# A transformer and mixture-of-experts kernel on one core: biases of q, k and v folded into weights made on chip, one more head on VectorE, shared first products in another order

## The chip, the core and the metric

The kernel runs on one core of a Trainium2 chip. Five engines work side by side and meet at semaphores: PE (TensorE, matrix products), DVE (VectorE), ACT (ScalarE), POOL (GpSimd) and SP (SyncE, which here only issues DMAs). The metric is the device time of one execution in microseconds (us); the time of the kernel before is the median of three executions.

## The reference

Input is 16 x 512 tokens of 256 numbers in float32. What is computed, cut to what matters:

```python
xn = layernorm(layernorm(x)) * ln1_w + ln1_b          # the inner norm has no weights
q, k, v = xn @ wq + bq, xn @ wk + bk, xn @ wv + bv    # 16 heads of 16
fq, fk = elu(q) + 1, elu(k) + 1
kv = einsum('bhnd,bhne->bnde', fk, v)                 # sum over the heads h of one token
attn = einsum('bhnd,bnde->bhne', fq, kv) / (einsum('bhnd,bnd->bhn', fq, fk.sum(1)) + 1e-6)
x2 = layernorm(x) + attn @ wo + bo
x1 = x + x2 + gelu(LN2(x2) @ fc_w + fc_b) @ proj_w + proj_b
h = layernorm(x1)
out = x1 + shared(h) + sum over the top 2 of 8 experts of weight * expert(h)
# shared(h) = (silu(h @ sg_gate.T) * (h @ sg_up.T)) @ sg_down.T; an expert has the same form
```

Attention stays within a token: for each token the 16 heads of q meet the 16 heads of k and v, so it is elementwise work of 16 x 16 x 16 products, done on DVE and POOL and not on PE.

## The kernel before

The 8192 tokens go through in 16 blocks of 512, each of four tiles of 128 tokens. A block passes through a pipeline of stages, one per round of `body(c, j)`: in round c the attention of block c is computed (`core`), block c-1 gets its output product, LN2 and the MLP (`stage_b`), block c-2 is routed to experts and gets the first products of the shared expert (`stage_c`), and block c-3 gets the shared expert's last product and is stored (`stage_d`). Projections of the first three tiles of block c+1 stand in round c already (`more`). Rounds 0 to 18 take about the first 1140 us. Then the tokens, sorted by expert in HBM, go through the experts in 71 tiles of 256 rows. That second phase is not touched.

Every engine has its own list of instructions, written out by hand in the order in which it runs them, and waits at semaphores where it needs another's result. So an engine that waits holds up all that stands behind in its own list.

What the change and the prediction touch, by lines of the kernel before:

- PE, `project_x(c, u, part)` (L1448 on): part "T" transposes a tile u (L1456, identity as weights); part "P" multiplies it with `wqkv_sb` into PSUM, 512 columns for q and k and 256 for v (L1466), and then adds the biases with two bfloat16 products of `bias_rows_bf` and `bias_bf` (L1471), one of 512 and one of 256 columns. "P" waits for `pq_free`, with which DVE gives back the PSUM bank.
- PE, `body`: the output product with `wo_sb` (`to_tokens`, L1494, biases L1497), logits (L1626, 16 products of 8 columns), `down` (L1494 with `sgdn_sb`: the shared expert's last product, which waits for `shared_h`), the MLP's first product (L1548), its second (L1494 with `proj_sb`), and `shared_up` (L1641: six first products n = 0 to 5 of the shared expert, gate and up parts in turn).
- ACT, `take_x` (L669 on): takes a transposed tile from PSUM and applies LN1's weight and bias per column (L676, two instructions for the two halves of 128 columns). `take_qkv` (L687, L690, L700) takes q, k (as exp) and v. `take_shared` (L762) takes the six first products, the gate parts through Silu. Silu and exp need different function tables, so `table` (L772) and `table_exp_ln` (L776) load one.
- DVE, `heads` of a tile by `own_heads(u)`: 16, and for tile `SPLIT` = 2 only 16 - `POOL_HEADS`. Four long instructions per tile make its attention: `products_qk` (L1026), `sums_1` (L1035), `products_2` (L1050), `sums_2` (L1063). `residual_1` (L1144) adds the output product to the residual and waits for `wo_psum`. `weights` (L1211) waits for ACT's `gap_exp`. `features(c + 1, 0)` (L1002, L1007) writes `fqk_pool`, the tile that POOL does alone.
- POOL, `body`: products of that tile (`scores`, L537), sums by halving (L523, L533), `gate_shared` (L583: silu part times up part of the shared expert, whose end is `shared_h`), the second products (L544), the heads of tile SPLIT that are POOL's (`heads`), and eight scatters of rows to HBM (L574).

The lines that say the split and the biases:

```python
POOL_HEADS = 6
def own_heads(u):
    return HEADS - POOL_HEADS if u == SPLIT else HEADS
```

Of the kernel before, what the change touches and what calls it, by code (L numbers as in the profile page):

```python
# [56 lines left out]

POOL_TILE = 3
SPLIT = 2
POOL_HEADS = 6  # L60
RANKS_AT = 5
ORDER = (POOL_TILE, 0, 1, 2)
BIAS_ROWS = (0, 64, 96)
# [4 lines left out]
def build(nc, x, wqkv, b_tok, ln1w, ln1b, ln2w, ln2b, wo, fc_w, fc_b, proj_w, gate_w, sg_up, sg_down,  # L68
          experts, out):
    ctx = ExitStack()  # L70
    with ctx:
        def sb(name, shape, dt=FP32):
            return ctx.enter_context(nc.sbuf_tensor(name, shape, dt))

        def sem(name):
            return ctx.enter_context(nc.semaphore(name))
# [5 lines left out]


        wqkv_sb = sb("wqkv_sb", [P, KC, 3 * D])
        wo_sb = sb("wo_sb", [P, KC, D])
        fc_sb = sb("fc_sb", [P, KC, MLP])
        proj_sb = sb("proj_sb", [P, FCH, D])
# [5 lines left out]
        ln_sb = sb("ln_sb", [P, 4, KC])  # L93
# [5 lines left out]
        ident = sb("ident", [P, P])  # L99
# [98 lines left out]
            (0, HEADS * HH), (HEADS * HH, 2 * D), (HEADS * HH + 2 * D, D), (HEADS * HH + 3 * D, HEADS * HEADS)))  # L198
        first_v2 = first_v2.rearrange("p (h e) -> p h e", h=HEADS)
        first_s2 = first_s2.rearrange("p (h g) -> p h g", h=HEADS)  # L200
        first_v = sg_u[:, 0, 0:D].rearrange("p (e g) -> p e g", e=HD)


# [51 lines left out]
        xnT_ready = sem("xnT_ready")  # L255
        qkv_psum = sem("qkv_psum")
        qkv_taken = sem("qkv_taken")
        feat_ready = sem("feat_ready")
        pq_free = sem("pq_free")
        pool_v_used = sem("pool_v_used")  # L260
# [111 lines left out]
        def announce(eng, ins, s, value):  # L372


            ins.then_inc(s, 1)
            eng.wait_ge(s, value)
# [17 lines left out]
        def stages(c):  # L394

            return (not isinstance(c, int) or c < BLOCKS, not isinstance(c, int) or c < BLOCKS - 1,
                    *(not isinstance(c, int) or s <= c < BLOCKS + s for s in (1, 2, 3)))

        block = ctx.enter_context(nc.Block())

# [266 lines left out]
        def _(act):  # L667
            a = nc.scalar

            def take_x(c, u):  # L670

                n = 4 * c + u
                wait(act, xT_psum, n + 1)
                wait(act, qkv_psum, n - 1)
                for k in range(KC):
                    ins = a.activation(xnT[u % 2][:, k, :], p_xT[:, k * P:(k + 1) * P], ACT.Identity,  # L676
                                       bias=ln_sb[:, 1, k:k + 1], scale=ln_sb[:, 0, k:k + 1])
                ins.then_inc(xnT_ready, 1)

            def take_qkv(c, u):  # L680
# [137 lines left out]
            def token_numbers(c, j):  # L818
# [2 lines left out]
                act.wait_ge(tok_moved, c - 1)  # L821
                a.activation(rows[j % 2][:, :, C_TOK], tok[:], ACT.Copy).then_inc(tok_written, 1)

            def take_sums(i, dst, src):

                act.wait_ge(first_pool, i + 1)
                a.activation(dst.rearrange("p h g -> p (h g)"), src[:, 0:HEADS * HEADS], ACT.Copy).then_inc(s_taken, 1)

            def body(c, j):
# [62 lines left out]
                if stage_b and (more or not core):  # L892
                    for k in range(2):
                        ln3_sums(c, j, k)
                        ln3_finish(c, k)
                if more:
                    take_qkv(c + 1, 1)
                if stage_c:
                    table(ACT.Silu)
                    take_shared(c, range(2))  # L900
                    if stage_b and not core:
                        normed_rows(c, j + 1)
                    if core and not more:
                        ln3_sums(c, j, 0)
                    take_shared(c, range(2, 4))
                    if core and not more:
                        ln3_sums(c, j, 1)
                if more:
# [64 lines left out]
        def _(dve):  # L973
# [110 lines left out]
            def first_block():  # L1084
# [50 lines left out]
                announce(dve, ins, attn_ready, 1)  # L1135
                dve.sem_inc(pq_free, 1)

            def residual_1(c):
# [83 lines left out]
            def body(c, j):  # L1222
# [17 lines left out]
                if core:  # L1240
                    totals(1, den_1[:, 0:HEADS])
                    products_2(c, 1, False)
                if stage_c:
                    choose(c, j)
                if core:
# [73 lines left out]
            done(v.memset(neg_1[:], -1.0))  # L1319
            done(v.memset(eps_1[:], EPS))  # L1320
            done(v.memset(block_1[:], float(BLOCK)))
            done(v.memset(eps_2[:], EPS * EPS))
            announce(dve, v.memset(act_tmp[:], 0.0), tmp_ready, 1)
            dve.wait_ge(pool_const, 4)
# [121 lines left out]
        def _(pe):  # L1446
            t_ = nc.tensor

            def project_x(c, u, part):

                n = 4 * c + u
                if part == "T":
                    wait(pe, xhat_ready, TPB * c + u + 1)
                    wait(pe, xnT_ready, n)
                    for k in range(KC):
                        ins = t_.transpose(p_xT[:, k * P:(k + 1) * P],  # L1456
                                           xin[:, ORDER[u], k * P:(k + 1) * P], ident[:])
                    ins.then_inc(xT_psum, 1)
                else:
                    wait(pe, xnT_ready, n + 1)  # L1460
                    wait(pe, qkv_taken, n)
                    wait(pe, pq_free, n - 1)
                    parts = ((p_qk[u % 2], 0, 512), (p_v, 512, 768))
                    for bnk, lo, hi in parts:
                        for k in range(KC):
                            t_.matmul(bnk[:, 0:hi - lo], xnT[u % 2][:, k, :], wqkv_sb[:, k, lo:hi],  # L1466
                                      start=k == 0, stop=False)
                    if isinstance(n, int) and n == 0:
                        pe.wait_ge(bias_ready, 1)
                    for bnk, lo, hi in parts:  # L1470
                        ins = t_.matmul(bnk[:, 0:hi - lo], bias_rows_bf[:], bias_bf[:, lo:hi],  # L1471
                                        start=False, stop=True)
# [28 lines left out]
            def body(c, j):  # L1501
# [23 lines left out]
                                    lambda t: wait(pe, rows_ready, TPB * (c - 2) + t + 1))  # L1525
                if core:
                    project_x(c, 2, "P")
                if stage_c:
                    logits(c)
                if stage_d:  # L1530
# [24 lines left out]
                if stage_b:  # L1555
                    wait(pe, gelu_ready, FCH * c - 1)
                    wait(pe, out_ready, c - 2)
                    if stage_c and more:
                        wait(pe, ranks_read, c - 1)

                    def next_x(u):
                        project_x(c + 1, u, "T")
                        if u == 1:
                            project_x(c + 1, 0, "P")
                    to_tokens(hid, FCH, proj_sb, (p_b0, p_b1), 4 * D, proj_psum,
                              at_last_chunk=lambda: wait(pe, gelu_ready, FCH * c),
                              between=next_x if more else None, per_bank=True)
                elif more:
                    project_x(c + 1, 0, "T")
                    project_x(c + 1, 1, "T")  # L1570
# [218 lines left out]
```

## Time and profile before

| | |
|---|---|
| time, median of 3 executions | 1746.89 us (1745.64 to 1747.42) |
| profiled execution, its own time | 1744.85 us |
| its span, first to last instruction | 1742.7 us |
| PE busy | 1680.7 us (96%) |
| DVE, POOL busy | 1166.9 us each (67%) |
| ACT busy | 904.1 us (52%) |
| granted PE clock, mean | 0.985 of full |

DVE and POOL are busy in the rounds of the first phase and nearly idle in the experts' phase, so their share of the whole span says little: a round is to be read by itself. Rows of the timeline give start, duration, engine, line and operation, tiles written and read, the number merged, and in brackets how long the engine had been idle before and what ended that.

### The profile page before, as it was taken

The numbers are of one execution on the slowest core, as the hardware profiler recorded it, in microseconds if no ns is written. First come the engines' busy times: TensorE is split into PE (matmuls) and PEld (weight loads), VectorE is DVE, ScalarE is ACT, GpSimd is POOL, SyncE is SP. The second block draws the span as 40 slices with busy tenths as digits, with TensorE's granted clock in tenths as the row PEclk, the third lists the DMA queues.
The fourth block names the chain that finished last, engine by engine and source line by source line (L and its number), as shares of the span: only waits on it lengthen the run. The fifth ranks groups of instructions, "written<-read, shape, count | busy, mean of one in ns | idle before, by whom it ended". The sixth has DMA issues, their size and how long they took to land.

```text
span 1742.7 us, 25628 instructions
## 1 busy us (share of the span) xinstructions
PE 1680.7 (96%) x7243; PEld 1227.5 (70%) x7289; DVE 1166.9 (67%) x1968; ACT 904.1 (52%) x2240; POOL 1166.9 (67%) x624
## 2 busy tenths in 40 slices
PE   6899999999999999999999998989999999999997
PEld 4555666666666666666666665578888888888886
DVE  7989999999999999999999993322222222222221
ACT  4356667667667667667667646522322322332322
POOL 5769889889889889889889881413333343343343
PEclk9898999999999999999999999999999999999999
DMA  4302211211211211111111111367777777777764
GB/s 151 116 13 61 62 49 37 62 49 36 61 49 36 61 49 36 59 50 36 54 55 37 37 49 37 92 169 162 165 154 160 165 157 156 167 158 156 168 158 78
DMA packets 89455, 157.20 MB, mean 90 GB/s; under 512 B 8896, under 2 KB 72128, under 8 KB 89024
## 3 DMA queue, kind: packets, MB, share of 16 engines
q1 hardware_dynamic: 60512, 112.58, 20.9%
q0 software_dynamic: 28896, 44.06, 14.9%
q8 instruction: 21, 0.34, 0.1%
q14 instruction: 26, 0.21, 0.0%
HBM read 101.79 MB, written 48.56 MB: 86 GB/s over the span
## 4 chain that ended last, share of the span: by engine, by line
PE 89%; ACT 5%; DVE 2%; issue 2%; DMA 1%; POOL 1%; SPq 1%; POOLq 0%; ACTq 0%; DVEq 0%
PE p_b L1494 17%; PE p_b L1548 13%; PE p_b L1698 10%; PE p_b L1709 10%; PE p_b L1641 8%; PE p_q L1698 7%; PE p_q L1466 6%; PE p_v L1698 4%; PE p_v L1466 3%; PE p_b L1480 2%; PE p_xT L1685 2%; PE p_xT L1626 2%; ACT rows L706 1%; ACT xmid L706 1%; PE p_b L1588 1%
## 5 line engine op out<-in xcount | busy, mean ns | idle before, releaser
L654 POOL DMA_INDIRECT out_rows<-prod_pool,prod x142 | 221.4, 1559 | 387.9 <-ACT prod_pool L949 357.5
L523 POOL TENSOR_TENSOR prod_pool<-prod_pool 128x2048 f32<-128x2048 f32 (+1 forms) x180 | 347.9, 1933 | 14.1
L1548 PE MATMUL p_b<-bT,fc_sb 128*128 128x512 f32 x512 | 231.5, 606 | 1.3 <-ACT bT L865 1.3
L1494 PE MATMUL p_b<-proj_sb,hid 128*128 128x256 f32 x1024 | 230.5, 379 | 0.0
L1494 PEld LDWEIGHTS p_b<-proj_sb,hid 128*128 128x128 f32 x1024 | 189.6, 190 | 29.4 <-issue 0.5
L1026 DVE TENSOR_TENSOR prod<-p_q,eqk 128x4096 f32<-128x4096 f32 (+1 forms) x47 | 184.0, 3914 | 5.3 <-DVE attn L1076 1.0
L1698 PE MATMUL p_b<-prod,exp_up 128*128 128x256 f32 x840 | 187.1, 379 | 0.0
L1063 DVE TENSOR_REDUCE qkv<-prod 128x256 f32<-128x4096 f32 (+1 forms) x47 | 183.7, 3910 | 1.6
L1050 DVE TENSOR_TENSOR prod<-p_q,v_dve 128x2048 f32<-128x2048 f32 (+2 forms) x60 | 177.4, 2956 | 1.5
L574 POOL DMA_INDIRECT rows_sorted<-rows,slot x128 | 125.7, 982 | 78.5 <-issue 34.5
L1035 DVE TENSOR_REDUCE p_q<-prod 128x128 f32<-128x2048 f32 (+2 forms) x60 | 177.4, 2957 | 1.1
L1548 PEld LDWEIGHTS p_b<-bT,fc_sb 128*128 128x128 f32 x512 | 97.9, 194 | 113.6 <-issue 106.4
L1641 PE MATMUL p_b<-x3T,sgup_sb 128*128 128x512 f32 x384 | 172.0, 593 | 0.3 <-ACT sg_g L762 0.3
L1698 PEld LDWEIGHTS p_b<-prod,exp_up 128*128 128x128 f32 x840 | 156.9, 190 | 19.9
L1428 DVE TENSOR_TENSOR prod_pool<-prod,p_b 128x256 f32<-128x256 f32 x105 | 44.3, 422 | 178.6 <-ACT prod L941 136.4
L537 POOL TENSOR_TENSOR prod_pool<-fqk_pool 128x4096 f32<-128x4096 f32 x16 | 120.8, 7550 | 41.5 <-DVE fqk_pool L1007 40.9
L949 ACT ACTIVATE prod_pool<-p_b,prod 128x256 f32<-128x256 f32 x142 | 59.6, 471 | 160.4 <-PE p_b L1709 158.1
L1698 PE MATMUL p_q<-prod,exp_up 128*128 128x256 f32 x576 | 132.7, 384 | 0.8 <-ACT prod L935 0.8
L870 ACT ACTIVATE hid<-p_b,fcb_sb 128x512 f32<-128x512 f32 x128 | 88.0, 687 | 83.1 <-PE p_b L1548 83.1
L1466 PE MATMUL p_q<-wqkv_sb,xnT 128*128 128x512 f32 x256 | 124.4, 609 | 5.9 <-DVE prod L1050 3.1
L544 POOL TENSOR_TENSOR prod_pool<-s_pool,v_pool 128x4096 f32<-128x4096 f32 x16 | 126.1, 7883 | 0.1
L1641 PEld LDWEIGHTS p_b<-x3T,sgup_sb 128*128 128x128 f32 x384 | 69.7, 190 | 75.8 <-issue 71.3
(208 smaller groups left out, 2988.6 us busy)
## 6 DMA issues: line engine op xcount, KB each, us to landing
exp_up<-in_experts SPq DMA_DIRECT2D x71, 768.0 KB
prod<-rows_sorted SPq DMA_DIRECT2D x71, 260.0 KB
xin<-in_x SPq DMA_DIRECT2D x16, 512.0 KB, 3.4
xres<-in_x SPq DMA_DIRECT2D x16, 512.0 KB
xres<-xmid POOLq DMA_DIRECT2D x16, 512.0 KB, 4.6
out_rows<-x SPq DMA_DIRECT2D x16, 512.0 KB, 2.9
exp_dn<-in_experts SPq DMA_DIRECT2D x8, 384.0 KB, 5.8
out_rows<-prod_pool,prod POOLq DMA_INDIRECT x142, 3.8
```

Source lines behind the costliest of these rows:

```text
L523: done(g.tensor_tensor(prod_pool[:, at:at + n * w], prod_pool[:, at:at + n * w], prod_pool[:, at + n * w:at + 2 * n * w], ALU.add))
L654: pool.indirect_dma_start(out=out[:, :], out_offset=bass.IndirectOffsetOnAxis(ap=tok_i[j][:, a:a + 1], axis=0), in_=yg[j][:, a * D:(a + 1) ...
L1026: return v.tensor_tensor(at[:, 0:n * HH].rearrange("p (h g d) -> p h g d", h=n, g=HEADS), p_qk[u % 2][:, 0:n * HD].rearrange("p (h d) -> p ...
L1035: done.later(v.tensor_reduce(p_qk[u % 2][:, lo * HEADS:hi * HEADS], prod[:, lo * HH:hi * HH].rearrange("p (a d) -> p a d", d=HD), AX.X, AL ...
L1050: ins = v.tensor_tensor(prod[:, lo * HH:hi * HH].rearrange("p (h e g) -> p h e g", h=n, e=HD), p_qk[u % 2][:, lo * HEADS:hi * HEADS].rearr ...
L1063: done.later(v.tensor_reduce(qkv[u % 2][:, 0:n].rearrange("p h e -> p (h e)"), prod[:, 0:n * HH].rearrange("p (a g) -> p a g", g=HEADS), A ...
L1466: t_.matmul(bnk[:, 0:hi - lo], xnT[u % 2][:, k, :], wqkv_sb[:, k, lo:hi], start=k == 0, stop=False)
L1494: ins = t_.matmul(o, src[:, k, t * P:(t + 1) * P], w[:, k, :], start=k == 0, stop=bias_at is None and k == chunks - 1)
L1548: ins = t_.matmul(bnk[:], fc_sb[:, k, f * P:(f + 1) * P], bT[:, k, :], start=k == 0, stop=k == KC - 1)
L1641: ins = t_.matmul(bnk[:], sgup_sb[:, k, lo:lo + P], x3T[:, k, :], start=k == 0, stop=k == KC - 1)
L1698: ins = t_.matmul(gu_banks[j][i][:, part * TILE:(part + 1) * TILE], exp_up[j][:, at:at + P], xgT[j][:, c * TILE:(c + 1) * TILE], start=c = ...
L1709: ins = t_.matmul(y_bank[:, h * D:(h + 1) * D], hgT[j][:, i * TILE + h * P:i * TILE + (h + 1) * P], exp_w(e, at, at + D), start=i == 0, st ...
```

## The change

The double layer norm leaves rows whose mean is 0. So for tiles n = 4c+u of 12 and more (`FOLDED` = 3 blocks) `take_x` no longer applies LN1's weight and bias, but adds 1 to every element, in one instruction instead of two, and PE multiplies with `wfold`: `wqkv` times LN1's weight, plus in every row the same vector, (bias + (ln1_b - ln1_w) @ wqkv) / 256. A row of mean 0 gives nothing with equal rows; the added 1 gives back the column sums. The two bias products per tile are left out. `wfold` is made once, by ACT in round 0 (`fold_parts`), PE and DVE in round 1 (`fold`). `POOL_HEADS` is 5 instead of 6, so DVE does 11 heads of tile 2 instead of 10. In rounds that have a next block, PE issues the shared first products in groups of three, one and two, where it had two, two and two, around the projection of tile 1 and the transposes of tile 2; ACT takes three of them before it takes q, k and v of tile 1, with a table load for Silu before and one for exp behind.

```diff
-POOL_HEADS = 6
+POOL_HEADS = 5
+FOLDED = 3
...
+        def folded(n):
+            return not isinstance(n, int) or n >= 4 * FOLDED
...
             def take_x(c, u):
...
-                for k in range(KC):
-                    ins = a.activation(xnT[u % 2][:, k, :], p_xT[:, k * P:(k + 1) * P], ACT.Identity,
-                                       bias=ln_sb[:, 1, k:k + 1], scale=ln_sb[:, 0, k:k + 1])
+                if folded(n):
+                    ins = a.activation(xnT[u % 2][:].rearrange("p k t -> p (k t)"), p_xT[:, 0:D], ACT.Identity,
+                                       bias=one_1[:, 0:1])
...
+            def fold_parts():
+                for k in range(KC):
+                    a.activation(fold_d[:, k:k + 1], ln_sb[:, 0, k:k + 1], ACT.Identity, scale=-1.0,
+                                 bias=ln_sb[:, 1, k:k + 1]).then_inc(fold_diff, 1)
+                    a.activation(wfold[:, k, :], wqkv_sb[:, k, :], ACT.Copy, scale=ln_sb[:, 0, k:k + 1]
+                                 ).then_inc(fold_in, 1)
+                act.wait_ge(fold_diff, KC)
+                for k in range(KC):
+                    a.activation(fold_w[:, k, :], ident[:], ACT.Identity, scale=0.0, bias=fold_d[:, k:k + 1]
+                                 ).then_inc(fold_in, 1)
...
+                if first:
+                    fold_parts()
+                if more and stage_c:
+                    table(ACT.Silu, 2)
+                    take_shared(c, range(3))
+                    table_exp_ln()
                 if more:
                     take_qkv(c + 1, 1)
                 if stage_c:
                     table(ACT.Silu)
-                    take_shared(c, range(2))
+                    if not more:
+                        take_shared(c, range(2))
...
-                    take_shared(c, range(2, 4))
+                    take_shared(c, range(3 if more else 2, 4))
...
+            def fold():                                  # DVE, in round 1
+                dve.wait_ge(fold_psum, 1)
+                dve.wait_ge(fold_in, 2 * KC)
+                for k in range(KC):
+                    for bnk, lo, hi in ((p_b0, 0, 512), (p_b1, 512, 768)):
+                        ins = v.scalar_tensor_tensor(wfold[:, k, lo:hi], bnk[:, 0:hi - lo], 1.0 / D, wfold[:, k, lo:hi],
+                                                     ALU.mult, ALU.add)
...
+                    w = wfold if folded(n) else wqkv_sb   # PE, project_x part "P"
...
+                    if not folded(n):
...
+            def fold():                                  # PE, in round 1 before the transposes of LN2's rows
+                pe.wait_ge(fold_in, 2 * KC)
+                wait(pe, attnT_ready, KC)
+                for bnk, lo, hi in ((p_b0, 0, 512), (p_b1, 512, 768)):
+                    for k in range(KC):
+                        t_.matmul(bnk[:, 0:hi - lo], fold_w[:, k, :], wqkv_sb[:, k, lo:hi], start=k == 0, stop=False)
+                    ins = t_.matmul(bnk[:, 0:hi - lo], bias_rows_bf[:], bias_bf[:, lo:hi], start=False, stop=True)
+                ins.then_inc(fold_psum, 1)
...
                 if stage_c and stage_b:
-                    shared_up(c, range(2))
+                    shared_up(c, range(3))
                 if more:
                     project_x(c + 1, 1, "P")
                 if stage_c and stage_b:
-                    shared_up(c, range(2, 4))
+                    shared_up(c, range(3, 4))
```

PE, from the shared first products (`x3T`, `sgup_sb`) over the projection of tile 1 (`xnT`, with `wqkv_sb` or `wfold`) to the transposes of the attention (`attn`), before:

```order
L1641 MATMUL p_b<-x3T,sgup_sb 128x512 x4
L1466 MATMUL p_q<-wqkv_sb,xnT 128x512 [waits pq_free,qkv_taken,xnT_ready]
L1466 MATMUL p_q<-wqkv_sb,xnT 128x512
L1466 MATMUL p_v<-wqkv_sb,xnT 128x256 x2
L1471 MATMUL p_q<-bias_bf,bias_rows_bf 128x512
L1471 MATMUL p_v<-bias_bf,bias_rows_bf 128x256
L1641 MATMUL p_b<-x3T,sgup_sb 128x512 [waits x1_read]
L1641 MATMUL p_b<-x3T,sgup_sb 128x512
L1641 MATMUL p_b<-x3T,sgup_sb 128x512 [waits x1_read]
L1641 MATMUL p_b<-x3T,sgup_sb 128x512
```

and with the change:

```order
L1709 MATMUL p_b<-x3T,sgup_sb 128x512 x4
L1709 MATMUL p_b<-x3T,sgup_sb 128x512 [waits x1_read]
L1709 MATMUL p_b<-x3T,sgup_sb 128x512
L1519 MATMUL p_q<-wfold,xnT 128x512 [waits pq_free,qkv_taken,xnT_ready]
L1519 MATMUL p_q<-wfold,xnT 128x512
L1519 MATMUL p_v<-wfold,xnT 128x256 x2
L1709 MATMUL p_b<-x3T,sgup_sb 128x512 [waits x1_read]
L1709 MATMUL p_b<-x3T,sgup_sb 128x512
```

The third first product (two rows) has moved ahead of the projection, and the two bias rows are gone.

ACT at the same place, with the change, from the last step of LN3's scales (`rs_c`) to the take of tile 2 (`xnT`); before, `eqk` and `v_dve` came right behind `rs_c`, then one table load and four rows with `sg_g` and `sg_u`:

```order
L824 ACTIVATE rs_c<-rs_c,mean_c 128x1
L789 ACT_TABLE_LOAD
L789 ACTIVATE act_tmp<-act_tmp 128x1
L779 ACTIVATE sg_g<-p_b 128x512 [waits up_psum]
L779 ACTIVATE sg_u<-p_b 128x512 [waits up_psum]
L779 ACTIVATE sg_g<-p_b 128x512 [waits up_psum]
L793 ACT_TABLE_LOAD
L704 ACTIVATE eqk<-p_q,neg 128x512 [waits feat_ready,qkv_psum]
L717 ACTIVATE v_dve<-p_v 128x256 [waits pq_free]
L789 ACT_TABLE_LOAD
L789 ACTIVATE act_tmp<-act_tmp 128x1
L779 ACTIVATE sg_u<-p_b 128x512 [waits up_psum]
```

The take of q, k and v of tile 1 has two table loads and three takes of shared products ahead of it.

## Rows read from the trace of the kernel before

**Rows 1.** Busy time by stretch: one round, then stretches of either clock level.

```profile
core 0: us, PE busy (x) PEld busy (x) DVE busy (x) ACT busy (x) POOL busy (x), PEclk, DMA share, GB/s
473.36:539.22 65.86, 65.29 (x268) 42.48 (x272) 62.67 (x81) 45.26 (x115) 60.21 (x30) 1.00 0.16 48
...
142.40:152.60 10.20, 8.03 (x15) 3.69 (x16) 9.91 (x24) 6.59 (x14) 10.12 (x3) 0.50 0.28 53
152.60:1060.50 907.90, 895.38 (x3660) 581.45 (x3699) 856.64 (x1088) 614.85 (x1539) 815.75 (x413) 1.00 0.16 47
1060.50:1067.40 6.90, 6.90 (x20) 5.73 (x20) 2.29 (x21) 2.88 (x8) 0.98 (x1) 0.51 0.40 76
...
1115.20:1118.60 3.40, 3.26 (x22) 2.18 (x21) 2.48 (x18) 1.69 (x3) 0.00 (x0) 0.50 0.00 0
```

**Rows 2.** The timeline of DVE: its longest wait in a steady round.

```profile
533.41 1.28 DVE L1144 TENSOR_TENSOR xmid<-xmid,p_b 128x512 f32<-128x512 f32 x2 [1.40 <-PE p_b L1497]
```

**Rows 3.** Timelines of POOL and PE: from POOL's tile to the shared expert's last product.

```profile
518.23 7.55 POOL L537 TENSOR_TENSOR prod_pool<-fqk_pool 128x4096 f32<-128x4096 f32 x1 [0.32 <-DVE fqk_pool L1007]
...
535.20 3.44 POOL L583 TENSOR_TENSOR sg_g<-sg_g,sg_u 128x1536 f32<-128x1536 f32 x1 [0.17 <-POOL s_pool L533]
...
537.37 1.85 PE L1626 MATMUL p_xT<-gate_sb,x3T 128*128 128x8 f32 x16
539.08 2.19 PE L1494 MATMUL p_b<-sgdn_sb,sg_g 128*128 128x256 f32 x9
```

**Rows 4.** The timeline of PE: biases of one tile, and what follows.

```profile
520.05 0.38 PE L1471 MATMUL p_q<-bias_bf,bias_rows_bf 128*128 128x512 bf16 x1
...
520.37 3.60 PE L1641 MATMUL p_b<-x3T,sgup_sb 128*128 128x512 f32 x8
```

**Rows 5.** DVE's instructions by form, 210 to 1000 us: busy, mean ns of one.

```profile
L1026 DVE TENSOR_TENSOR prod<-p_q,eqk 128x4096 f32<-128x4096 f32 x24 | 106.2, 4425 | 2.0
...
L1026 DVE TENSOR_TENSOR prod<-p_q,eqk 128x2560 f32<-128x2560 f32 x12 | 33.9, 2825 | 1.6
...
L1063 DVE TENSOR_REDUCE qkv<-prod 128x160 f32<-128x2560 f32 x12 | 33.8, 2820 | 0.4
```

**Rows 6.** Timelines of ACT and DVE: the take of tile 1, and a table switch.

```profile
520.57 0.69 ACT L687 ACTIVATE eqk<-p_q,neg 128x512 f32<-128x512 f32 x1 [2.20 <-PE p_v L1471]
...
521.55 1.28 ACT L772 ACT_TABLE_LOAD   x1
...
522.96 0.58 ACT L762 ACTIVATE sg_g<-p_b 128x512 f32<-128x512 f32 x1
...
524.45 0.42 DVE L1002 SCALAR_TENSOR_TENSOR eqk<-eqk,p_q 128x256 f32<-128x256 f32 x1 [0.17 <-DVE attn L1076]
```

**Rows 7.** Timelines of ACT, PE and DVE: idle time in rounds 0 and 1.

```profile
65.35 0.69 ACT L687 ACTIVATE eqk<-p_q,neg 128x512 f32<-128x512 f32 x1 [15.76 <-PE p_v L1471]
...
80.22 2.17 PE L1480 MATMUL p_b<-ident,hid 128*128 128x128 f32 x8 [5.13 <-ACT hid L706]
...
119.92 0.69 DVE L1159 TENSOR_TENSOR x<-xres,p_b 128x512 f32<-128x512 f32 x1 [2.65 <-PE p_b L1497]
```

**Rows 8.** The timeline of PE: the wait for the last block's attention.

```profile
1050.96 1.09 PE L1480 MATMUL p_b<-ident,attn 128*128 128x128 f32 x8 [2.48 <-DVE attn L1076]
```

**Rows 9.** The timeline of PE: waits next to logits, outside the steady rounds.

```profile
143.92 2.17 PE L1480 MATMUL p_b<-ident,hid 128*128 128x128 f32 x8 [2.16 <-ACT hid L706]
...
1059.19 2.33 PE L1626 MATMUL p_xT<-gate_sb,x3T 128*128 128x8 f32 x16 [1.16 <-ACT x3T L753]
...
1112.00 1.92 PE L1626 MATMUL p_xT<-gate_sb,x3T 128*128 128x8 f32 x16 [1.16 <-ACT x3T L753]
```

**Rows 10.** Timelines of ACT and DVE: the experts' weights, in a steady round and in round 2.

```profile
496.21 0.21 ACT L877 ACTIVATE gap_e<-gap 128x4 f32<-128x4 f32 x1
...
496.72 0.15 DVE L1211 TENSOR_SCALAR p_q<-gap_e 128x4 f32<-128x4 f32 x1
...
166.84 0.17 DVE L1211 TENSOR_SCALAR p_q<-gap_e 128x4 f32<-128x4 f32 x1 [0.84 <-ACT gap_e L877]
```

More of the change, by code:

```diff
@@ L84, in build @@
         wqkv_sb = sb("wqkv_sb", [P, KC, 3 * D])
+        wfold = sb("wfold", [P, KC, 3 * D])
+        one_1 = sb("one_1", [P, 1])
+        fold_d = sb("fold_d", [P, KC])
         wo_sb = sb("wo_sb", [P, KC, D])
@@ L200, in build @@
         first_s2 = first_s2.rearrange("p (h g) -> p h g", h=HEADS)
+        fold_w = sg_u[:, 1, 0:KC * P].rearrange("p (k n) -> p k n", k=KC)
         first_v = sg_u[:, 0, 0:D].rearrange("p (e g) -> p e g", e=HD)
@@ L257, in build @@
         qkv_taken = sem("qkv_taken")
+        fold_diff = sem("fold_diff")
+        fold_in = sem("fold_in")
+        fold_psum = sem("fold_psum")
+        fold_ready = sem("fold_ready")
         feat_ready = sem("feat_ready")
@@ L674, in take_x @@
                 wait(act, qkv_psum, n - 1)
-                for k in range(KC):
-                    ins = a.activation(xnT[u % 2][:, k, :], p_xT[:, k * P:(k + 1) * P], ACT.Identity,
-                                       bias=ln_sb[:, 1, k:k + 1], scale=ln_sb[:, 0, k:k + 1])
+                if folded(n):
+                    ins = a.activation(xnT[u % 2][:].rearrange("p k t -> p (k t)"), p_xT[:, 0:D], ACT.Identity,
+                                       bias=one_1[:, 0:1])
+                else:
+                    for k in range(KC):
+                        ins = a.activation(xnT[u % 2][:, k, :], p_xT[:, k * P:(k + 1) * P], ACT.Identity,
+                                           bias=ln_sb[:, 1, k:k + 1], scale=ln_sb[:, 0, k:k + 1])
                 ins.then_inc(xnT_ready, 1)
@@ L1136, in first_block @@
                 dve.sem_inc(pq_free, 1)
+            def fold():
[5 more added lines that the diff above has]
+                                                     ALU.mult, ALU.add)
+                        if k < KC - 1 or lo == 0:
+                            done.later(ins)
+                done.sync()
+                announce(dve, ins, fold_ready, 1)
             def residual_1(c):
@@ L1242, in body @@
                     products_2(c, 1, False)
+                if isinstance(c, int) and c == 1:
+                    fold()
                 if stage_c:
@@ L1321, in _ @@
             done(v.memset(block_1[:], float(BLOCK)))
+            done(v.memset(one_1[:], 1.0))
             done(v.memset(eps_2[:], EPS * EPS))
@@ L1463, in project_x @@
                     parts = ((p_qk[u % 2], 0, 512), (p_v, 512, 768))
+                    w = wfold if folded(n) else wqkv_sb
                     for bnk, lo, hi in parts:
                         for k in range(KC):
[L1466 to L1472, printed above, removed]
-                    ins.then_inc(qkv_psum, 1)
+                            ins = t_.matmul(bnk[:, 0:hi - lo], xnT[u % 2][:, k, :], w[:, k, lo:hi],
+                                            start=k == 0, stop=folded(n) and k == KC - 1)
+                    if not folded(n):
+                        if isinstance(n, int) and n == 0:
+                            pe.wait_ge(bias_ready, 1)
+                        for bnk, lo, hi in parts:
+                            ins = t_.matmul(bnk[:, 0:hi - lo], bias_rows_bf[:], bias_bf[:, lo:hi],
+                                            start=False, stop=True)
+                    ins.then_inc(qkv_psum, 1)
+            def fold():
+                pe.wait_ge(fold_in, 2 * KC)
+                wait(pe, attnT_ready, KC)
+                for bnk, lo, hi in ((p_b0, 0, 512), (p_b1, 512, 768)):
+                    for k in range(KC):
+                        t_.matmul(bnk[:, 0:hi - lo], fold_w[:, k, :], wqkv_sb[:, k, lo:hi], start=k == 0, stop=False)
+                    ins = t_.matmul(bnk[:, 0:hi - lo], bias_rows_bf[:], bias_bf[:, lo:hi], start=False, stop=True)
+                ins.then_inc(fold_psum, 1)
             def transpose_block(src, banks, ready, tile_ready=None):
@@ L1527, in body @@
                     project_x(c, 2, "P")
+                if isinstance(c, int) and c == 1:
+                    fold()
                 if stage_c:
@@ L1557, in body @@
                     wait(pe, out_ready, c - 2)
+                    if isinstance(c, int) and c == 1:
+                        pe.wait_ge(fold_ready, 1)
                     if stage_c and more:
```

## The prediction

> **What bounds it now.** I first read the table of the profile: PE is busy 96% of the span, so I look for what PE waits for, and for who could take its place. The second view is busy time by stretch [rows 1]. Between about 210 and 1000 us the rounds repeat every 65.86 us; in the round shown PE is busy 65.29, DVE 62.67 and POOL 60.21. All three are close to the round, so a saving on one is worth what the next one leaves. PE is the longest: DVE's longest wait is for PE, 1.40 before the residual add [rows 2]. Without it DVE would need 65.86 - 1.40 = 64.46 a round.
>
> The third view is the timeline across engines, for the loop that comes next [rows 3]. POOL starts its own tile at 518.23, after waiting 0.32 for DVE's features of it, and ends the shared expert's product at 535.20 + 3.44 = 538.64. PE's `down` needs that product and starts at 539.08, right behind the logits. So POOL is 0.44 ahead of PE there, and no more.
>
> The fourth view is the granted clock in the same table of stretches [rows 1]: 1.00 (2.4 GHz) through all steady rounds, 152.6 to 1060.5, and 0.50 (1.2 GHz) in some short stretches outside them.
>
> **What the change does to PE.** Per folded tile the two bias products go. They take PE from 520.05 to 520.37, 0.32 [rows 4]. Four tiles a round make 1.28: PE's round becomes 64.58 if nothing else holds it. The regrouping adds no product; it puts 1.8 (half of 3.60 [rows 4]) of work ahead of tile 1's projection.
>
> **To DVE.** One more head in four long passes of tile 2. From 10 to 16 heads a pass grows from 2.825 to 4.425 us [rows 5], 0.267 a head; the passes are alike at 10 heads (2.820 for the last), so four make 1.07. The small ones around (one row more, one row less) cancel within 0.02. DVE's round becomes 64.46 + 1.07 = 65.53. That alone leaves only 0.33 of PE's 1.28.
>
> **To POOL.** It loses a sixth of its two rounds on tile 2's heads. That stands behind the product in [rows 3], and POOL already waits for DVE at the start of its own tile, so it becomes idle time there and starts nothing earlier. POOL's start even moves back with DVE's extra head.
>
> **The loop through POOL.** Residual add, DVE's passes, POOL's tile, `shared_h`, PE's `down`, MLP, projections, output product, residual add: this loop spans two rounds, 131.72. DVE's stretch in it gains 1.07. PE's stretch loses three tiles' biases, 0.96; tile 2's stands ahead of `down`. The lead of 0.44 can go but for some 0.06 of latency: 0.38. So 131.72 + 1.07 - 0.96 - 0.38 = 131.45, or 65.73 a round. This is longer than DVE's 65.53, so it sets the round if the clock stays up: 0.13 less than now.
>
> **Where PE's freed time goes.** PE then has 65.73 - 64.58 = 1.15 to wait per round, and it waits at `down`, just behind the logits, which are 16 products of 8 columns in 1.7 us. So a stretch with hardly any columns grows from 1.7 to 2.9 us. The trace has three places where logits and a wait stand side by side: waits of 2.16, 1.16 and 1.16 us [rows 9]. All three were followed by a half clock: 142.4 to 152.6, 1060.5 to 1067.4, 1115.2 to 1118.6 [rows 1]. The twelve steady rounds, with logits and no wait, had none. I take it that the new wait brings some of this into the steady rounds.
>
> **Its price.** Work issued at half clock takes twice as long, so the shortest such stretch, 3.4 us, loses 1.7; the longest, 10.2, loses 5.1. I take the shortest, because heavy products follow `down` at once. The delay passes on: PE's MLP runs late, ACT's `gap_e` comes late, and DVE's `weights` waits for it. There ACT is 496.72 - 496.42 = 0.30 ahead [rows 10]; with the change DVE comes there 0.80 later (three of the four longer passes) and PE's `down` about 0.8 later after the residual add, so the lead stays. In round 2, after the half clock of 142.4, DVE waited 0.84 at this place [rows 10]. So a drop costs 1.7 - 0.3 = 1.4 of the round. How many rounds? None would be the steady rounds' record, all twelve the record of the three places. The wait is near the 1.16 ones, but a drop makes PE late and shortens the next wait; I take six. Bounds: 0 and 12 x 1.4 = 16.8.
>
> **The rest.** ACT's six instructions in round 0 stand in an idle stretch of 15.76. PE's six fold products, about 1.7 (two of 512 columns at 3.60 / 8 = 0.45 [rows 4], two of 256 at half of that, and the biases' 0.32), stand in an idle 5.13. DVE's four fold instructions, about 2.1 by its 0.69 for a like one of 512 columns and 0.42 for 256, and the longer passes' 1.07 find 2.65 of waiting before the residual add of round 1 and some more before it [rows 6, 7]. So the fold costs nothing; without that cover it would cost up to 3. Round 2 has two folded tiles: -0.64. In the last block PE waits 2.48 for DVE's attention [rows 8], so the longer passes count there in full: +1.07. ACT's take in one instruction only helps. The tables: see the fourth rival.
>
> **Sum.** Twelve rounds at -0.13 make -1.6; -0.64; +1.07; six drops of 1.4 make +8.4. Together +7.2. The profiled execution took 1744.85 (1742.7 of it the span), 2.04 under the median of the runs. 1744.85 + 7.2 = 1752.1, as a median 1754.1.
>
> **Rivals.**
> 1. The clock stays up. For: a wait of 1.15 is short, and falls where PE was idle before on other occasions without harm (2.48 before the last attention [rows 8] had no half clock right behind it). Against: the three places of [rows 9]. Then -1.6 - 0.64 + 1.07 = -1.2: 1745.7, no change that shows (a measurement of this kernel can tell about 0.2%, 3.5 us).
> 2. The change pays. If POOL's product came early enough, DVE's 65.53 alone would set the round: 12 x 0.33 = 4.0 less, in sum -3.6, 1743.3, at the edge of what shows. All of PE's saving, 52 x 0.32 = 16.6, would give 1730.3, but DVE's own 65.53 excludes it, unless part of its waiting hides in the gaps between its instructions. Decides: whether DVE's wait for the output product disappears.
> 3. The clock falls in all rounds, or for longer: up to 16.8 - 1.2, 1762.5, and some more with longer stretches. This is my forecast at its upper end.
> 4. ACT becomes late with tile 1. Three takes and two table loads now stand ahead of it. With 0.58 a take and 1.41 and 1.28 for the two switches (521.55 to 522.96, and the load alone) that is 4.4; 2.20 of it was idle time [rows 6]. The take would end about 2.2 later than 521.5, at 523.7, some 0.7 ahead of DVE's use at 524.45. Were a switch to cost twice its load, 1.28 more each, DVE would wait 1.9 a round: 12 x (65.53 + 1.9 - 65.86) = 19 more, about 1766. Against it: after the load at 521.55 the first take follows in 1.41, with no room for a second cost. The Trainium skill (ScalarE: Activation LUTs, "What ACT_TABLE_LOAD costs") gives a load of about 1283 ns and a drain of about 1380, 2.66 us for every switch to another set; by it, as an estimate, each of the two switches would cost 1.38 more and the kernel would come out near rival 4's time. The load agrees with the 1.28 of the row, the drain does not show.
> 5. The change doesn't do what it says: the biases' products go by the order of PE's instructions, so I give this nothing.
>
> **Chances.** Forecast with its upper end (1 and 3 of the clock's cases that show): 0.58. Few drops or none, within 0.2%: 0.26. The change pays by more than 0.2%: 0.13 (DVE alone at its edge, or gaps that I read wrong). ACT late: 0.03. So faster 0.13, same 0.26, slower 0.61. The range reaches from just under DVE's own bound, 1742, to twelve drops with some longer ones, 1766. The likeliest case alone holds 1750 to 1763.
>
> **What would show it.** Right: DVE's wait of 1.40 shrinks to some tenths, bias products are gone from tiles 12 on, PE waits about 1 us before `down` for POOL's product, and the granted clock between 200 and 1000 us is under 1.00 in part, with DVE waiting for `gap_e` in those rounds. The regrouped products show no new wait of DVE for tile 1. Wrong: a clock of 1.00 throughout with rounds of 65.7 (rival 1) or 65.5 (rival 2); or rounds near 64.6, then my DVE sum fails; or DVE waiting for ACT's take of tile 1 (rival 4).

## The result, and the profile after the change

The changed kernel takes 1775.25 us (median of 4 executions, 1773.38 to 1777.0) against 1747.16 for the kernel before: ratio 1.0162, 95% interval 1.0144 to 1.0179. It is slower by 28, and lies above the forecast of 1754.1 and its range (1742 to 1766). The profiled execution took 1777.0, its span 1775.3.

The rounds tell where the time is. From one residual add to the next, the twelve rounds from 204.4 us on take 65.85 to 66.17 before, and now 68.51, 68.88, 68.78, 69.08, 65.88, 68.43, 68.71, 68.91, 68.78, 69.35, 65.68, 68.34. So ten rounds lost about 3, and the two others took what the forecast's sum gave without a drop of the clock (65.73). The round after them, the last full one, takes 67.25 for 62.42. From here on a quick round is one of about 65.8, a slow one one of over 68, and a drop is a stretch of PE at half clock. The table of stretches shows one quick round, one slow one, and pieces of the slow one (columns as in [rows 1]):

```profile
479.65:545.54 65.89, 64.04 (x265) 42.13 (x263) 63.76 (x81) 46.56 (x114) 58.25 (x31) 1.00 0.17 48
613.96:682.67 68.71, 66.16 (x264) 43.14 (x263) 63.84 (x81) 46.32 (x114) 57.96 (x31) 0.98 0.15 46
617.20:620.60 3.40, 1.85 (x17) 1.75 (x15) 3.33 (x6) 2.16 (x6) 3.37 (x1) 1.00 0.00 0
621.60:625.00 3.40, 3.40 (x10) 2.69 (x9) 3.33 (x6) 0.68 (x4) 3.40 (x2) 0.50 0.69 133
```

DVE and POOL are as busy in the slow round as in the quick one; PE is 2.1 busier, at half clock (1.2 GHz) from 621.6 to 625.0. The same table over the whole steady stretch finds eleven such pieces, nine of 3.4 and two of 6.8 us; before there was none ([rows 1]). The profiled execution is no exception: the mean granted clock of the four executions is 0.973 to 0.977, that of the kernel before, in the executions taken beside e1 to e4, 0.985 to 0.988. Three of the pieces:

```profile
212.00:215.40 3.40, 3.40 (x10) 2.69 (x9) 3.37 (x6) 0.72 (x4) 3.40 (x2) 0.50 0.72 140
...
416.80:423.60 6.80, 6.24 (x15) 4.98 (x16) 6.50 (x21) 2.10 (x7) 6.07 (x3) 0.50 0.41 77
...
1031.20:1034.60 3.40, 3.40 (x9) 2.70 (x8) 3.40 (x6) 0.86 (x4) 3.40 (x2) 0.50 0.67 129
```

What stands ahead of each is, in the timeline of PE, logits and then a wait for POOL's product (compare [rows 3], where `down` followed the logits at once). In four of the eleven the clock falls while PE still waits; two of the thirteen such waits, of 1.50 and 1.64, were followed by none:

```profile
617.20 1.85 PE L1694 MATMUL p_xT<-gate_sb,x3T 128*128 128x8 f32 x16
620.73 5.84 PE L1558 MATMUL p_b<-sgdn_sb,sg_g 128*128 128x256 f32 x18 [1.68 <-POOL sg_g L596]
```

The 18 products of `down` take 5.84; without a drop they take 4.15. In the list of waits three lines have grown:

```profile
DVE p_q L1260 <- ACT gap_e L906: 23.4, 13, 5.1
...
PE p_b L1558 <- POOL sg_g L596: 20.7, 13, 1.7
...
DVE x L1208 <- remote: 11.8, 8, 1.6
```

The timeline of DVE in that round shows the first and the last of them:

```profile
645.68 0.17 DVE L1260 TENSOR_SCALAR p_q<-gap_e 128x4 f32<-128x4 f32 x1 [1.65 <-ACT gap_e L906]
...
665.08 0.69 DVE L1208 TENSOR_TENSOR x<-xres,p_b 128x512 f32<-128x512 f32 x1 [1.43 <-remote]
```

1.65 + 1.43 = 3.08 is about what the slow round (68.71) has over 65.7. Eight of the ten slow rounds show both waits. In the two with a drop of 6.8 us the first is 2.4 and of the second 0.3 and 0.4 are left. The wait of [rows 2] before the residual add is gone: L1193 waits twice in all, outside these rounds. The first wait was in the forecast; the second was not. "Remote" means that no instruction's record explains when the semaphore rose. It is the one that PE's last bias product of the MLP raises, and that product's record ends 2.3 earlier:

```profile
662.49 0.27 PE L1561 MATMUL p_b<-bias_bf,bias_rows_bf 128*128 128x256 bf16 x1
```

The trace's own list of this semaphore's updates has it at 665.06, and in the slow rounds 1.1 to 2.5 behind the product's end; in the quick one it came at once (0.01). At that time POOL issues its scatters; the eighth is the last before POOL's own tile:

```profile
617.24 3.44 POOL L596 TENSOR_TENSOR sg_g<-sg_g,sg_u 128x1536 f32<-128x1536 f32 x1 [0.16 <-POOL s_pool L546]
...
662.66 0.96 POOL L587 DMA_INDIRECT rows_sorted<-rows,slot  x1 [0.30 <-issue]
669.01 7.55 POOL L550 TENSOR_TENSOR prod_pool<-fqk_pool 128x4096 f32<-128x4096 f32 x1 [5.40 <-DVE fqk_pool L1043]
```

### The profile page after: what moved, and what is told of

Same layout as the page of the kernel before. It is cut to its first block, busy times and chain, and to the rows that moved or that the text cites. A ratio compares the mean times of both kernels' runs of the same rounds, so it can differ in the third digit from the quotient of the medians.

```text
span 1775.3 us, 25481 instructions
## 1 busy us (share of the span) xinstructions
PE 1693.0 (95%) x7188; PEld 1239.0 (70%) x7195; DVE 1186.4 (67%) x1973; ACT 921.4 (52%) x2233; POOL 1133.8 (64%) x624
## 4 chain that ended last, share of the span: by engine, by line
PE 49%; POOL 32%; issue 8%; DVE 6%; ACT 2%; DMA 1%; SPq 1%; POOLq 1%; another core or an unknown queue 0%; DVEq 0%; ACTq 0%
POOL prod_pool L536 13%; PE p_b L1766 10%; PE p_b L1777 10%; PE p_q L1766 7%; PE p_b L1558 6%; POOL prod_pool L550 6%; POOL prod_pool L557 5%; PE p_b L1614 5%; POOL rows_sorted L587 4%; PE p_v L1766 3%; POOL sg_g L596 2%; PE p_xT L1753 2%; PE p_q L1519 1%; DVE prod L1062 1%; DVE p_q L1071 1%
## 5 line engine op out<-in xcount | busy, mean ns | idle before, releaser
L536 POOL TENSOR_TENSOR prod_pool<-prod_pool 128x2048 f32<-128x2048 f32 (+1 forms) x180 | 333.8, 1855 | 14.1
L1062 DVE TENSOR_TENSOR prod<-p_q,eqk 128x4096 f32<-128x4096 f32 (+1 forms) x47 | 188.0, 3999 | 4.6
L1099 DVE TENSOR_REDUCE qkv<-prod 128x256 f32<-128x4096 f32 (+1 forms) x47 | 187.7, 3994 | 1.6
L1086 DVE TENSOR_TENSOR prod<-p_q,v_dve 128x2048 f32<-128x2048 f32 (+2 forms) x60 | 181.4, 3023 | 1.5
L1071 DVE TENSOR_REDUCE p_q<-prod 128x128 f32<-128x2048 f32 (+2 forms) x60 | 181.5, 3024 | 1.1
L1558 PE MATMUL p_b<-sgdn_sb,sg_g 128*128 128x256 f32 x384 | 113.5, 458 | 22.1 <-POOL sg_g L596 20.7
```

The lines of the kernel that those rows point to most:

```text
L536: done(g.tensor_tensor(prod_pool[:, at:at + n * w], prod_pool[:, at:at + n * w], prod_pool[:, at + n * w:at + 2 * n * w], ALU.add))
L1062: return v.tensor_tensor(at[:, 0:n * HH].rearrange("p (h g d) -> p h g d", h=n, g=HEADS), p_qk[u % 2][:, 0:n * HD].rearrange("p (h d) -> p ...
L1071: done.later(v.tensor_reduce(p_qk[u % 2][:, lo * HEADS:hi * HEADS], prod[:, lo * HH:hi * HH].rearrange("p (a d) -> p a d", d=HD), AX.X, AL ...
L1099: done.later(v.tensor_reduce(qkv[u % 2][:, 0:n].rearrange("p h e -> p (h e)"), prod[:, 0:n * HH].rearrange("p (a g) -> p a g", g=HEADS), A ...
L1558: ins = t_.matmul(o, src[:, k, t * P:(t + 1) * P], w[:, k, :], start=k == 0, stop=bias_at is None and k == chunks - 1)
```

## Experiments

The theory under test: PE's freed time waits behind the logits, the clock falls there, and the delay goes on to DVE through `gap_e` and, a second time, through the semaphore that is late under the scatters. The rivals: the extra head, or the shared products in groups of three with their table loads, cost the time by themselves. No version leaves out part of the computation.

The ratio is to the kernel before as measured beside the run.

| run | median us | ratio to before, 95% interval | drops, 200 to 1035 us |
|---|---|---|---|
| the change | 1775.25 | 1.0144 to 1.0179 | 11 |
| e1: filler products | 1749.48 | 1.0012 to 1.0031 | 0 |
| e2: gate first | 1745.10 | 0.9986 to 1.0005 | 0 |
| e3: six heads on POOL | 1747.62 | 0.9999 to 1.0019 | 5 |
| e4: scatters later | 1755.39 | 1.0031 to 1.0064 | 7 |
| e5: six heads, gate early | 1737.21 | 0.9947 to 0.9976 | 3 |
| e6: no fold | 1762.68 | 1.0085 to 1.0160 | 5 |
| e7: groups of two | 1774.90 | 1.0158 to 1.0211 | 10 |
| e9: six heads, gate first | 1734.83 | 0.9924 to 0.9958 | 0 |
| e10: e5 and a filler | 1737.45 | 0.9937 to 0.9970 | 0 |
| e11: six heads, fillers | 1748.08 | 1.0003 to 1.0022 | 0 |

**e1. Keep PE at work in the wait.**

```diff
 if stage_c: logits(c)
+if stage_d and core:
+    for _ in range(2):
+        t_.matmul(p_b0[:], ident[:], sgup_sb[:, 0, 0:512], start=True, stop=True)
 if stage_d: down(c, ...)
```

> The change, with two more products of 512 columns (0.43 us each) between logits and `down` in PE's list, whose results nobody reads. If the clock is the cause (PE's wait next to the logits brings the half clock): the wait shrinks from 1.7 to under 0.5, the granted clock stays at 1.00 from about 154 to 1055 us, all rounds take 65.7 to 66.0 as the two rounds without a drop do in the trace of the change, and the ten slow rounds lose 2.9 each: 1775 - 29 = 1746. If something else costs the time (the extra head, ACT's tables, the order of the shared products), two more products in PE's list can only add: 1775 or more, rounds still near 68.8.

1749.48: 25.8 of the 28.1 came back although PE has more to do. The timeline of PE shows the two products as four instructions, 1.84 in all where I had reckoned 0.86, so they fill the wait completely:

```profile
471.23 1.85 PE L1697 MATMUL p_xT<-gate_sb,x3T 128*128 128x8 f32 x16
472.93 1.96 PE L1598 MATMUL p_b<-sgup_sb,ident 128*128 128x512 f32 x4
474.77 4.15 PE L1558 MATMUL p_b<-sgdn_sb,sg_g 128*128 128x256 f32 x18
```

The clock stays up in the whole steady stretch, and most rounds take 65.94, now PE's own length:

```profile
463.60:529.70 66.10, 65.74 (x267) 42.75 (x267) 64.03 (x81) 46.41 (x114) 58.20 (x31) 1.00 0.16 48
```

`down` starts no earlier than in the change, 6.81 after the residual add (474.77 against 467.96) for 6.77 (620.73 against 613.96). So it was not the lateness of `down` that cost the time but the half clock behind it. DVE's extra head and ACT's table loads are all still there, so neither costs the time by itself. The two longest rounds, of 66.8, have the wait for "remote" (1.09 and 1.31) without a drop.

**e2. Take the wait away.**

```diff
+if stage_d and stage_c: gate_shared(c)
 if core:
     wait(pool, attn_ready, c)
     done(halve(flat(s_pool[:, 0:HEADS, :])))
-if stage_d and stage_c: gate_shared(c)
```

> The change, with POOL's `gate_shared` moved ahead of the halving of its own tile, so that `shared_h` comes some 8 us earlier and `down` finds it done. Clock theory: no wait of PE behind the logits, PE's freed time moves to another place (output product or `weights`), granted clock 1.00 in the steady rounds, rounds between DVE's own 65.53 and 65.86, time 1742 to 1747. Rival (the clock is not the cause): 1775 as the change, since neither DVE's nor ACT's work is touched. A third way: the wait for ACT's takes makes POOL late for its second products and a later reader waits, then rounds grow with the clock at 1.00.

1745.10, no difference to before that shows, rounds of 65.4 to 66.2 and no drop: the change without its wait is worth about what rivals 1 and 2 gave, DVE's bound of 65.53 and a little more. POOL pays for the early gate with a wait for ACT's takes, which its idle time covers:

```profile
527.03 3.48 POOL L596 TENSOR_TENSOR sg_g<-sg_g,sg_u 128x1536 f32<-128x1536 f32 x1 [1.69 <-ACT sg_u L779]
```

**e3. The sixth head back on POOL** (`POOL_HEADS = 6`; fold and groups stay).

> The change with the sixth head back on POOL (fold and order of the shared products stay). If the extra head on DVE is the cause: about 1746 or less. Clock theory: PE has some 0.9 to spare (64.58 against POOL's own 65.5) and still waits for POOL's product behind the logits, so the clock still drops in most rounds; but POOL's scatters end about 1.3 later than with five heads, so the second wait of DVE (1.43 before the second half of L1208) goes: some ten rounds of about 67.4 instead of 68.8, about 1760.

A miss in size: 1747.62 for 1760. The time alone is what the first case, the head as the cause, had given. But in e1 the head stays and the time comes back, so the head matters by making POOL's product late. Drops fell in five of the rounds, not in most, and the others took 65.2 to 65.7, less than before. A round with a drop takes 66.8 to 67.5, and no wait for "remote" is left. The fold without the head, then, gains a little less in its quick rounds than its drops cost: the twelve rounds take 794.1 together, before 790.8.

**e4. The scatters two microseconds later.**

```diff
 heads(c)
+done(g.tensor_tensor(prod_pool[:, 0:880], prod_pool[:, 0:880], prod_pool[:, 880:1760], ALU.add))
 if stage_c: scatter(c, j)
```

> The change, with one more addition of 880 elements on POOL (about 2 us, on data that is dead) ahead of its eight scatters, where POOL has 2.3 to 5.4 idle behind them. What is asked is the wait of 1.43 of DVE before the second half of L1208, whose PE semaphore comes 2.2 to 2.5 us after the product's end in the rounds with a drop. If it is the last of POOL's scatters that holds the semaphore up (it comes 1.4 after the issue of the eighth ends): the scatters now end behind it, the wait is gone, the drops stay (ten or so), slow rounds 68.8 - 1.4 = 67.4, time about 1775 - 8 x 1.4 = 1763. If PE itself is late there: the wait stays and the time is 1775 or a little more.

The wait for "remote" is gone in all rounds, as the timelines of DVE and POOL in a round with a drop show:

```profile
653.00 0.69 DVE L1209 TENSOR_TENSOR x<-xres,p_b 128x512 f32<-128x512 f32 x1
```

```profile
642.19 2.06 POOL L640 TENSOR_TENSOR prod_pool<-prod_pool 128x880 f32<-128x880 f32 x1
...
654.08 0.96 POOL L587 DMA_INDIRECT rows_sorted<-rows,slot  x1 [0.30 <-issue]
```

PE's product ends there at 652.04 and the eighth scatter is issued at 654.08, so the end of the scatters lies behind it. The trace's list has the semaphore's update at 652.98, still 0.93 late, but DVE was ready for it only at 652.92 and lost less than 0.1. The time fell by 20, more than the 12 expected, since the drops became fewer as well. The twelve rounds together take 798.6, 10.2 more than twelve of 65.7, with six drops in them: 1.7 a drop on average. In the change they take 819.3, with ten drops: 3.1 a drop. The difference of 1.4 is near the second wait of 1.43, which so depends on where POOL's scatters stand. How a scatter holds up another engine's semaphore was not tried, nor whether it does so outside of a profiled execution.

**e5. Six heads, and the gate behind the first of POOL's four halvings.**

```diff
 if core:
     wait(pool, attn_ready, c)
-    done(halve(flat(s_pool[:, 0:HEADS, :])))
+    halve_once(0, D, 8)
 if stage_d and stage_c: gate_shared(c)
+if core:
+    done(halve(flat(s_pool[:, 0:HEADS, :]), first=4))
```

> The fold with the sixth head back on POOL, and `gate_shared` put behind the first of the four halvings of POOL's own tile (so that it need not wait for ACT's takes, as it did 1.69 in each round when it stood ahead of them all). PE needs 64.58 a round, DVE 64.46, and the run with six heads had rounds of 65.2 where no drop fell. If the wait behind the logits is what brings the drops, there are none and all rounds take about 65.2: 12 x 0.66 = 7.9 less than before, 1738. If PE's time to spare brings the drops wherever it is waited, some stay and the time is near that of the run with six heads, 1747.

1737.21 as expected, but not quite in the way expected: the quickest rounds take 64.4, under the 65.2 that I took for the bound, and three drops are left behind waits of 0.8 to 1.5.

**e6. No fold** (all tiles keep the bias products; the head and the groups stay).

> The change without the fold: all tiles keep their bias products, the extra head and the order of the shared products stay. Clock theory: PE needs 65.86 a round as before, the loop through POOL takes (131.72 + 1.07 - 0.38) / 2 = 66.2, so PE waits only 0.35 behind the logits: no drops or few, rounds of 66.2, 1746 + 12 x 0.34 = 1750. If the head or the order of the shared products by themselves cost what was lost: near 1775.

Neither: 1762.68 (1756.84 to 1768.99). Quick rounds take 65.9 to 66.7, but five drops stand in the steady stretch and a slow round takes 68.5 to 69.1, with the wait for "remote" in four of them. PE's waits behind the logits that a drop followed were 0.4 to 0.7, in this round 0.54, and that was enough, while four of 0.7 were followed by none:

```profile
609.84 1.85 PE L1694 MATMUL p_xT<-gate_sb,x3T 128*128 128x8 f32 x16
612.23 5.83 PE L1558 MATMUL p_b<-sgdn_sb,sg_g 128*128 128x256 f32 x18 [0.54 <-POOL sg_g L596]
```

So the extra head, with the groups of three, makes POOL's product late even when the fold frees nothing on PE, and costs 19 (1743.37 for the kernel before, beside this run). The fold lengthens the wait and doubles the drops. The head with neither fold nor groups of three was not run.

**e7. Groups of two** (order of the shared products, ACT's takes and tables as before).

> The change with the shared first products back in three groups of two, and ACT's takes and table loads in their old places; fold and extra head stay. If the groups of three cost time (ACT late, or PE's wait moved by them), clearly under 1775, by up to 20. If they are neutral, as the clock theory has it: 1775 within 4, drops in nearly all rounds.

The time is the change's, but by another road. Behind the logits PE waits 0.5 at most; it waits in front of tile 1's projection, for DVE to give the PSUM bank back, between products of 512 columns on both sides. In seven rounds the clock falls there, behind waits of 1.9 to 2.5, while five waits of 1.4 to 1.8 at this place were followed by no drop:

```profile
659.78 1.45 PE L1704 MATMUL p_b<-x3T,sgup_sb 128*128 128x512 f32 x3
663.36 2.63 PE L1514 MATMUL p_q<-wfold,xnT 128*128 128x512 f32 x4 [2.13 <-DVE prod L1081]
```

```profile
664.50:667.90 3.40, 3.40 (x7) 2.03 (x6) 3.37 (x2) 0.16 (x1) 3.40 (x1) 0.50 0.00 0
```

So "neutral" was right in time and wrong in kind: the groups of three took that wait away, and PE waits behind the logits instead.

**e9, e10, e11. The fold without the head.** Three more versions with six heads on POOL: e9 puts the gate ahead of all halvings (e2's edit), e10 adds half of e1's filler to e5, e11 adds all of it to e3.

> Six heads on POOL and `gate_shared` ahead of all halvings of POOL's own tile. The version with the gate behind the first halving still had waits of 0.8 to 1.5 behind the logits and three drops in the steady rounds. If POOL's wait for ACT's takes (1.69 a round with five heads) stays, POOL needs 64.4 + 1.7 = 66.1 a round, no drops: 1748. If POOL, later with six heads, finds the takes done, PE's wait behind the logits is gone and all rounds take 64.4 to 64.7: 1743 - 12 x 1.3 = 1728 to 1732.

> Six heads, the gate behind the first halving, and one product of 512 columns (0.43) between logits and `down`, whose result nobody reads. If the wait behind the logits brings the three drops that are left, they go (2.2 each, 6.6), and the product adds at most 0.43 to the rounds in which PE does not wait: 1737 - 6.6 + 12 x 0.2 = 1733. If the drops come from elsewhere they stay: 1737 to 1742.

> Six heads, the gate in its old place, two products of 512 columns between logits and `down`. With six heads alone the clock dropped in five of the steady rounds and the others took 65.2. Clock theory: no drops; PE now needs 64.6 + 0.86 = 65.4 a round, which sets it: 1746 - 12 x 0.45 = 1741. Against it: drops as with six heads alone, then 1747 or more.

e9 takes 1734.83, 0.59% less than before, and is the best of all, though above the 1728 to 1732 of the second case. POOL finds ACT's takes done, `down` follows the logits, and no drop falls in the steady stretch:

```profile
463.52 1.85 PE L1694 MATMUL p_xT<-gate_sb,x3T 128*128 128x8 f32 x16
465.23 4.13 PE L1558 MATMUL p_b<-sgdn_sb,sg_g 128*128 128x256 f32 x18
```

```profile
200.00:1035.00 835.00, 820.83 (x3364) 539.54 (x3363) 804.00 (x1031) 583.27 (x1415) 766.45 (x384) 1.00 0.16 48
```

Its rounds are 64.4 to 64.7 in the first half and 65.3 to 66.1 later, where PE waits 1.6 to 1.9 for ACT's `bT` ahead of the output product; no drop followed those waits. e10 has no drops either, but the filler product costs PE some 0.9 where I took 0.43: rounds of 65.07 and 1737.45, a miss of 4. By the same slip e11 takes 1748.08 for 1741: no drops, rounds of 65.9. With six heads, filling the wait costs about what the drops cost (1747.62 and 1748.08; 1737.21 and 1737.45). Moving the gate ahead costs less than either.

## Why the prediction was wrong, step by step

The place of the wait, the clock that follows it and the path to DVE were forecast rightly. Two terms of the sum failed: how often the clock falls (six for ten) and what a fall costs (1.4 for 3.1).

- **The engines' sums** held. The bias products are gone, and PE is busy 64.04 in a quick round for 65.29 before, 1.25 less where the sum had 1.28; DVE's passes at 11 heads take 3.09 (columns as in [rows 5]), 0.267 a head over [rows 5] at 10:

```profile
L1062 DVE TENSOR_TENSOR prod<-p_q,eqk 128x2816 f32<-128x2816 f32 x12 | 37.1, 3092 | 1.6
```

- **The loop of 65.73** held where no drop fell: 65.88 and 65.68. The round of 65.53 by DVE alone showed in e2, nearly.
- **The place of the wait and what follows it** held: behind the logits, with the half clock right after it. In the two rounds that follow a quick one the wait was 1.21 and 1.31, near the 1.15 forecast; in the others 1.5 to 1.7. That PE's freed time makes the wait is only half of it: without the fold (e6) it is still 0.5 to 0.7 in most rounds, from the late product alone.
- **"I take six" drops** failed: there were ten in twelve rounds, though the choice of the shortest stretch was right for nine drops of the eleven to 1035 us. The reason given was that a drop makes PE late and so shortens the next wait. It does not, since the delay does not stay on PE: DVE takes it over at `gap_e`, POOL's own tile starts later with it (55.1 after the residual add, 669.01 against 613.96, for 51.8 in a quick round), and POOL's next product is as late as PE. The next wait is as long as the last (1.61, 1.70, 1.70, 1.66 in four rounds in turn), and longer than behind a quick round.
- **"1.4 a drop"** failed by its missing half. The first wait of DVE is 1.65 where the sum had 1.7 less 0.3; e4, where only it is left, lost 1.7 a drop. The other 1.4 is the wait at L1208, a term that the sum left at nothing. Two shifts bring it. POOL, with a head less, "starts nothing earlier", the prediction said; it starts its scatters 0.7 earlier, 39.7 after the residual add (653.67 against 613.96) for 40.4 before (507.98 against 533.41 - 65.86), while PE's last MLP product comes 2.2 later behind the drop, at 48.5 for 46.4. So their last one, which ended 3.7 behind that product before (517.90 against 514.19), now ends 0.9 behind it, and the semaphore is late just when DVE asks for it.
- **The sum.** DVE's two new waits, added up from its timeline, are 16.7 before `weights` in ten rounds and 11.8 at L1208 in eight, 28.5 of the 30.9 by which the twelve rounds exceed twelve of 65.7 (3.1 a drop; the sum had 8.4 for six). These 30.9, less the 2.4 by which twelve rounds of before exceed twelve of 65.7, make the 28.6 (rounded) by which these rounds are longer. The last full round adds 4.8, as it has a drop too (1031.2) where the sum had 1.07 for the longer passes alone, and the rest is 0.8 shorter; together 32.6, the two spans' difference.
- **The fold's cost** was taken too low on PE: 0.45 is the time of one record in [rows 4], and a float32 product of 512 columns shows as two, the slip of e1 again. The six products took 2.9 (75.71 to 78.61) for the 1.7 forecast. Idle time covered them all the same: the residual add of round 3 starts 0.3 later than before (204.41 for 204.12).
- **Rival 1 and rival 2** are about what the kernel does once the wait is filled or gone (e1, e2). **Rival 3** was nearly right in its count of drops (12, and ten came) and short in their price. **Rival 5** did not happen.
- **Rival 4** did not happen. Timeline of ACT, the switch ahead of the three takes:

```profile
668.68 0.48 ACT L824 ACTIVATE rs_c<-rs_c,mean_c 128x1 f32<-128x1 f32 x2
669.17 1.28 ACT L789 ACT_TABLE_LOAD   x1
...
670.58 0.58 ACT L779 ACTIVATE sg_g<-p_b 128x512 f32<-128x512 f32 x1
```

The load starts right behind the instruction ahead of it (668.68 + 0.48), and the first take follows the load's start by 1.41, as in [rows 6]. The Trainium skill (ScalarE: Activation LUTs, "What ACT_TABLE_LOAD costs") adds a drain of about 1380 ns to each switch; the trace agrees with its 1283 for the load and shows no such drain here.

## What to carry to other kernels

When a change frees time on the busiest engine, look first where that time will be waited, and what stands next to it: a saving that is waited can cost more in clock than it was worth, here beside thin products (16 of 8 columns) and in e7 between wide ones, and moving the late product forward takes that loss back (1775 to 1745 here by moving one step of POOL). A saving came out where the head was left where it was as well (1735). Follow the delay around the loop before counting how often it strikes: if the engine that takes it over also feeds the wait, every round repeats it. And of an engine that becomes idle, look at what it now does earlier, its DMAs above all.

## What the runs showed of the hardware that was not expected

- A wait of 0.54 next to the logits (e6) was followed by the half clock, and four of 0.7 at the same place were not. Waits of 1.6 to 1.9 ahead of the output product (e9) were not either, and waits of 1.9 to 2.5 between wide products (e7) were. So the length of a wait does not tell by itself, nor the width of the products beside it; what does was not tried.
- Where PE's last MLP product ended near the issue of one of POOL's last scatters, the update of its semaphore came late: 1.1 to 2.5 us behind the product in the slow rounds of the change, in all ten of them 1.4 to 1.6 after the issue of the eighth scatter ended (665.06 against 663.62 in the round shown). A drop is not needed for it: in e1, without drops, it was 1.0 to 1.3 late in nine rounds and 2.0 and 2.2 in the two longest. The trace of the kernel before has such late updates in its rounds too, behind PE's shared products, where no engine waited for them.
